# Gate weights applied in the expert loop instead of behind it, in a one-core Trainium2 mixture-of-experts kernel

## The reference

```
pg = softmax(x @ Wg + bg);  gw, gi = top_k(pg, 2)             # 2 groups
pe = softmax(x @ We[g] + be[g]);  ew, ei = top_k(pe, 1)       # 1 expert in each
h  = gelu(x @ W1 + b1);  oe = h @ W2 + b2
out = sum over the 2 groups of  gw * ew * oe[chosen expert]
y  = out @ Wp + bp
return (y - mean) * rsqrt(var + eps) * gamma + beta            # added to the residual h
```

## Time and profile before

| | us |
|---|---|
| median of 3 runs | 294.81 |
| lowest and highest | 291.74, 296.34 |
| the profiled execution | 292.14 |
| its span in the profile | 290.3 |
| PE, DVE, ACT, POOL busy in it | 244.0, 131.6, 117.6, 124.8 |
| granted TensorE clock, mean | 0.908 |

### The profile page before, as it was taken

One profiled execution on the slowest core, in us unless ns is written; L12 is line 12 of the kernel. 1 busy time (PEld: TensorE's weight loads), 2 busy tenths in 40 slices (PEclk: granted clock), 3 DMA queues, 4 the chain that ended last, 5 costly groups with the idle time before them and its releaser, 6 DMA issues.

```text
span 290.3 us, 8714 instructions
## 1 busy us (share of the span) xinstructions
PE 244.0 (84%) x3013; PEld 226.9 (78%) x3013; DVE 131.6 (45%) x491; ACT 117.6 (41%) x436; POOL 124.8 (43%) x152
## 2 busy tenths in 40 slices
PE   7889993307379999999999999999999999369860
PEld 6677762006379999999999999999999999359750
DVE  7638887897053352332233233223322322212796
ACT  4355566215023344334424433443343344235960
POOL 5775550840524447556655664455445422200000
PEclk9999998555559999999999999999999999975995
DMA  4411441417998983899265265992595210085023
GB/s 78 81 29 24 107 110 44 119 46 180 238 248 200 260 216 93 212 229 221 79 148 164 59 154 154 237 228 77 133 234 164 71 54 27 28 250 186 28 81 110
DMA packets 55035, 39.20 MB, mean 135 GB/s; under 512 B 30131, under 2 KB 52165, under 8 KB 55013
## 3 DMA queue, kind: packets, MB, share of 16 engines
q1 hardware_dynamic: 50004, 26.51, 38.6%
q0 software_dynamic: 5008, 12.43, 15.0%
HBM read 30.36 MB, written 8.55 MB: 134 GB/s over the span
## 4 chain that ended last, share of the span: by engine, by line
PE 54%; issue 16%; DVE 10%; POOL 7%; DMA 5%; ACT 5%; POOLq 0%; SPq 0%; DVEq 0%; ACTq 0%
PE pA L1223 21%; PE pY L1236 18%; POOL y_rows L506 3%; POOL xg L500 3%; DMA xg<-x_rows,token_of 2%; PE pY L1143 2%; PE pX L1210 2%; PE pA L1159 2%; DMA ys<-y_rows 2%; DVE ys L1012 2%; PE pY L1144 2%; DVE ys L1017 2%; PE pY L1167 1%; PE pY L1087 1%; PE pY L1044 1%
## 5 line engine op out<-in xcount | busy, mean ns | idle before, releaser
L653 ACT ACTIVATE hT<-pA,b_s 128x128 f32<-128x128 f32 x234 | 64.7, 375 | 112.7 <-PE pA L1223 112.7
L1223 PE MATMUL pA<-xs,W_s 64*128 64x128 f32 x1404 | 90.0, 279 | 0.9 <-DVE xs L947 0.8
L1223 PEld LDWEIGHTS pA<-xs,W_s 64*128 64x128 f32 x1404 | 84.7, 192 | 1.1 <-issue 1.1
L1236 PE MATMUL pY<-W_s,hT 64*128 64x192 f32 x936 | 83.8, 323 | 1.0 <-DVE yo L976 1.0
L1236 PEld LDWEIGHTS pY<-W_s,hT 64*128 64x128 f32 x936 | 76.4, 187 | 1.1 <-issue 1.1
L506 POOL DMA_INDIRECT y_rows<-yo,dest_of x39 | 38.6, 990 | 74.1 <-DVE yo L976 74.1
L974 DVE COPY yo<-pY 128x192 f32<-128x192 f32 x39 | 14.0, 358 | 107.4 <-PE pY L1236 107.4
L500 POOL DMA_INDIRECT xg<-x_rows,token_of x41 | 39.9, 973 | 25.8 <-issue 9.0
L947 DVE COPY xs<-pX 128x192 f32<-128x192 f32 x82 | 25.3, 350 | 12.3 <-PE pX L1210 9.3
L463 POOL TENSOR_SCALAR x<-h,mu,rs 128x192 f32<-128x192 f32 x16 | 16.5, 1038 | 16.4 <-DVEq L856 8.3
L1210 PEld LDWEIGHTS pX<-ident,xg 64*128 64x128 f32 x246 | 16.3, 141 | 5.9 <-issue 5.9
(11 more groups left out here) (241 smaller groups left out, 265.7 us busy)
## 6 DMA issues: line engine op xcount, KB each, us to landing
W_s<-in_L_ffn_W_dram SPq DMA_DIRECT2D x30, 288.0 KB, 4.3
W_s<-in_L_ffn_W_dram SPq DMA_DIRECT2D x15, 576.0 KB
x_rows<-x SPq DMA_DIRECT2D x16, 192.0 KB, 2.7
ys<-y_rows SPq DMA_DIRECT2D x8, 384.0 KB, 5.7
out_dram<-ys SPq DMA_DIRECT2D x8, 192.0 KB, 1.9
xg<-x_rows,token_of POOLq DMA_INDIRECT x41
y_rows<-yo,dest_of POOLq DMA_INDIRECT x39
emb<-n_L_tok_embed_table_dram,ids POOLq DMA_INDIRECT x16, 2.5
```

The costliest lines, as they stand in the source:

```text
L653: ins = nc.scalar.activation(hT[v][:, j * P:(j + 1) * P], units(v, j), ACT.Gelu, bias=b1_s[u][:, j:j + 1])
L1223: mm = pe.matmul(units(v, n * HB + j), W1_s[u][rows, g, j * P:(j + 1) * P], xs[v][rows, g, :], start=(g == 0 and j == 0), stop=(g == DG - ...
L1236: mm = pe.matmul(pY[n][:, 0:D], hT[v][rows, j * P:(j + 1) * P], W2_s[u][rows, j, :], start=(j == 0), stop=(j == HC - 1))
```

## The change

The gate weights are written to a small table in DRAM, `w_rows`, one float for each pair. For each expert tile POOL gathers its 128 weights into a column of `wt`, with `weight_of` as index (the pair's number, or 0 for an empty place). DVE's two evictions multiply by that column, so that `y_rows` holds weighted rows, and the end stage adds two rows, a pair of tiles in one operation. ACT's scaling in the end stage goes away; it takes the root straight from the sums of squares. The order of the end stage is written anew: the mixes of two groups ahead, then the roots of a group with scale-downs of the group before between its steps. TensorE does two fillers in each skipped step and 27 behind the loop, and no longer waits for `moe_done`.

```diff
+    w_rows = nc.dram_tensor("w_rows", [K * TOKENS, 1], F32).ap()
...
+        weight_of = sb("weight_of", [P, ST], I32)
+        wt = sb("wt", [P, SLOTS])
+        root_eps = sb("root_eps", [P, 1])
...
-        ROOT_AT = {hi + 4: (g, lo, hi) for g, (lo, hi) in enumerate(GROUPS)}
+        ROOT_AT = {hi + 2: (g, lo, hi) for g, (lo, hi) in enumerate(GROUPS)}
...
+        w_store = w_rows.rearrange("(k p i) o -> p k (i o)", k=K, i=NT)
...
                 load_w2(e, t)
+                if t == SLOTS - 2:
+                    with nc.allow_non_contiguous_dma(reason="64-byte rows of weights"):
+                        sp.wait_ge(wk_known, 1)
+                        sp.dma_start(w_store, wk[:, :, :]).then_inc(w_out, 16)
             def renew(t, v, free):
...
             loaded = pool.value_load(steps_loaded[0:1, 0:1], min_val=AHEAD, max_val=ST)
+            def fetch_weight(t):
+                u = t % SLOTS
+                pool.indirect_dma_start(wt[:, u:u + 1], None, w_rows, bass.IndirectOffsetOnAxis(
+                    ap=weight_of[:, t:t + 1].bitcast(U32), axis=0)).then_inc(wt_in[u], 16)
             gather(SLOTS)
+            pool.wait_ge(w_out, 16)
+            for t in range(SLOTS):
+                fetch_weight(t)
             gather(SLOTS + 1)
...
                         scatter(t)
+                if t + SLOTS < FULL * SLOTS:
+                    fetch_weight(t + SLOTS)
+                elif t + SLOTS < ST:
+                    with pool.If(used > t + SLOTS):
+                        fetch_weight(t + SLOTS)
                 if SLOTS <= t < SLOTS + NT:
...
             load_table(ACT.Sqrt)
-            def scaled(i):
-                act.wait_ge(ys_in[i // CB], 16)
-                nc.scalar.activation(ys[:, 0, i, :], ys[:, 0, i, :], ACT.Copy, scale=wk[:, 0, i:i + 1]).then_inc(y1w, 1)
             def turned_mix(j):
...
                 nc.scalar.activation(ys[:, 1, i, :], ps_y(i), ACT.Square, accum_out=ss3[:, i:i + 1]).then_inc(squared, 1)
-            for i in range(NT + 5):
+            for i in range(NT + 3):
+                if i < NT:
+                    turned_mix(i)
                 if i in ROOT_AT:
                     g, lo, hi = ROOT_AT[i]
-                    act.wait_ge(var3, g + 1)
-                    nc.scalar.activation(sd3_s[:, lo:hi], ve3[:, lo:hi], ACT.Sqrt).then_inc(sd3, 1)
-                if i < NT:
-                    scaled(i)
+                    act.wait_ge(squared, hi)
+                    nc.scalar.activation(sd3_s[:, lo:hi], ss3[:, lo:hi], ACT.Sqrt, bias=root_eps[:, 0:1],
+                                         scale=0.25 / D).then_inc(sd3, 1)
                 if 2 <= i < NT + 2:
-                    turned_mix(i - 2)
-                if 4 <= i < NT + 4:
-                    square(i - 4)
+                    square(i - 2)
         @block.vector
...
             nc.vector.memset(unit[:, :], 1.0)
+            nc.vector.memset(root_eps[:, :], 0.25 * EPS)
             nc.vector.memset(idle[:, :], 1.0).then_inc(idle_set, 1)
...
                 hot_lanes(lo, lo + GROUP // 2)
+            link(V.reciprocal(pmax_v, r4[:, :]))
+            link(V.tensor_tensor(pg1[:, :, :], second[:, :, :], lg_t[:, :, 0, :], ALU.mult))
+            link(V.tensor_reduce(gmax2[:, :], pg1[:, :, :], AX.X, ALU.add))
+            link(V.tensor_tensor(gmax2[:, :], gmax2[:, :], pmax[:, :, 0], ALU.mult))
             dve.wait_ge(inv_mm, 1)
...
             link(V.tensor_tensor(inv[:, 3, :], inv[:, 1, :], inv[:, 0, :], ALU.add))
+            V.tensor_scalar(weight_of[:, :], inv[:, 3, :], -1.0, 0.0, ALU.add, ALU.max)
             spare = dump[:, :, :].rearrange("p a b -> p (a b)")
...
             turned(0, 0)
-            link(V.reciprocal(pmax_v, r4[:, :]))
-            link(V.tensor_tensor(pg1[:, :, :], second[:, :, :], lg_t[:, :, 0, :], ALU.mult))
-            link(V.tensor_reduce(gmax2[:, :], pg1[:, :, :], AX.X, ALU.add))
-            link(V.tensor_tensor(gmax2[:, :], gmax2[:, :], pmax[:, :, 0], ALU.mult))
             for k, (group, gw) in enumerate(((first[:, :, 0, :], pmax[:, :, 0]), (second[:, :, :], gmax2[:, :]))):
...
                 link(V.tensor_tensor(wk[:, k, :], wk[:, k, :], gw, ALU.mult))
+            dve.sem_inc(wk_known, 1)
             turned(1, 1)
...
                 at_least(dve, sent[u], 16 * i)
-                V.tensor_copy(yo[u][:, :], pY[0][:, 0:D]).then_inc(y_half, 1)
+                dve.wait_ge(wt_in[u], 16 * (i + 1))
+                V.tensor_scalar(yo[u][:, :], pY[0][:, 0:D], wt[:, u:u + 1], None, ALU.mult).then_inc(y_half, 1)
                 dve.wait_ge(y_half, t + 1)
-                V.tensor_tensor(yo[u][:, :], pY[1][:, 0:D], yo[u][:, :], ALU.add).then_inc(y_ev, 1)
+                V.scalar_tensor_tensor(out=yo[u][:, :], in0=pY[1][:, 0:D], scalar=wt[:, u:u + 1], in1=yo[u][:, :],
+                                       op0=ALU.mult, op1=ALU.add).then_inc(y_ev, 1)
             for u in range(SLOTS):
...
             dve.wait_ge(resid, NT)
-            def mix(i):
-                dve.wait_ge(y1w, i + 1)
-                V.scalar_tensor_tensor(out=mixw[:, i, 0:D], in0=ys[:, 1, i, :], scalar=wk[:, 1, i:i + 1],
-                                       in1=ys[:, 0, i, :], op0=ALU.mult, op1=ALU.add).then_inc(mix_done, 1)
+            def mix(b):
+                tiles = slice(CB * b, CB * b + CB)
+                dve.wait_ge(ys_in[b], 16)
+                V.tensor_tensor(mixw[:, tiles, 0:D], ys[:, 0, tiles, :], ys[:, 1, tiles, :], ALU.add).then_inc(mix_done, CB)
             def scaled_down(i):
...
                     V.tensor_tensor(fin[:, tiles, :], fin[:, tiles, :], h2[:, tiles, :], ALU.add).then_inc(fin_done, 1)
-            pending = []
-            for i in range(NT + 5):
-                if i in ROOT_AT:
-                    g, lo, hi = ROOT_AT[i]
-                    dve.wait_ge(squared, hi)
-                    V.tensor_scalar(ve3[:, lo:hi], ss3[:, lo:hi], 0.25 / D, 0.25 * EPS, ALU.mult, ALU.add).then_inc(var3, 1)
-                if i < NT:
-                    mix(i)
-                for j in pending[0:2 if i >= NT else 1]:
+            def roots_of(g, lo, hi, older):
+                tiles = slice(lo, hi)
+                dve.wait_ge(squared, hi)
+                link(V.tensor_scalar(ve3[:, tiles], ss3[:, tiles], 0.25 / D, 0.25 * EPS, ALU.mult, ALU.add))
+                for j in older[0:2]:
                     scaled_down(j)
-                pending = pending[2 if i >= NT else 1:]
-                if i in ROOT_AT:
-                    dve.wait_ge(sd3, g + 1)
-                    link(V.reciprocal(rs3[:, lo:hi], sd3_s[:, lo:hi]))
-                    link(V.tensor_tensor(tn3[:, lo:hi], rs3[:, lo:hi], ve3[:, lo:hi], ALU.mult))
-                    link(V.tensor_tensor(tn3[:, lo:hi], tn3[:, lo:hi], sd3_s[:, lo:hi], ALU.add))
-                    link(V.reciprocal(rs3[:, lo:hi], tn3[:, lo:hi]))
-                    pending = pending + list(range(lo, hi))
-            for j in pending:
+                dve.wait_ge(sd3, g + 1)
+                link(V.reciprocal(rs3[:, tiles], sd3_s[:, tiles]))
+                for j in older[2:3]:
+                    scaled_down(j)
+                link(V.tensor_tensor(tn3[:, tiles], rs3[:, tiles], ve3[:, tiles], ALU.mult))
+                for j in older[3:4]:
+                    scaled_down(j)
+                link(V.tensor_tensor(tn3[:, tiles], tn3[:, tiles], sd3_s[:, tiles], ALU.add))
+                link(V.reciprocal(rs3[:, tiles], tn3[:, tiles]))
+            mix(0)
+            mix(1)
+            older = range(0)
+            for g, (lo, hi) in enumerate(GROUPS):
+                if g < 3:
+                    mix(hi // CB)
+                    mix(hi // CB + 1)
+                roots_of(g, lo, hi, older)
+                older = range(lo, hi)
+            for j in older:
                 scaled_down(j)
...
             mm.then_inc(inv_mm, 1)
-            def keep_busy(scratch):
-                for _ in range(BUSY):
+            def keep_busy(scratch, count=BUSY):
+                for _ in range(count):
                     pe.matmul(scratch, ident[:, :], ident[:, :], start=True, stop=True)
...
                         down(i * SLOTS + u, u, LOAD2 * (i + 1))
-            pe.wait_ge(moe_done, 1)
-            keep_busy(pA[1][:, 0:P])
+                    with pe.Else():
+                        keep_busy(pA[1][:, 0:P], 2)
+            keep_busy(pA[1][:, 0:P], 3 * BUSY)
             for i in range(NT + 1):
...
```

More of the change, by code:

```diff
@@ L299, in lm_tower @@
         w1_in = [sem(f"w1_in{u}") for u in range(SLOTS)]
+        wk_known, w_out = sem("wk_known"), sem("w_out")
+        wt_in = [sem(f"wt_in{u}") for u in range(SLOTS)]
         w2_in = [sem(f"w2_in{u}") for u in range(SLOTS)]
@@ L306, in lm_tower @@
         ys_in = [sem(f"ys_in{b}") for b in range(B)]
-        y1w, mix_done, mixT_mm, mixT_ev, proj_mm, fin_done, fin_out = (sem(n) for n in (
-            "y1w", "mix_done", "mixT_mm", "mixT_ev", "proj_mm", "fin_done", "fin_out"))
```

(2 more changed lines are left out.)

## The result

The change is slightly slower. In 15 runs of each kernel the median is 295.36 us (292.42 to 298.07) against 294.27 (289.03 to 296.34) for the kernel before: 1.1 us more. By both the change is slower, and by less than 2%. The profiled execution of the change took 293.85 us, 1.71 more than that of before. The forecast was 293.5, with 0.4% gained.

A forecast was written before the change was run, and what follows sets the result against it. TensorE was taken to pace the expert loop at 4.2 us a tile. Approach 0, loop and evictions +0.05 and the end stage's walk together gave 1.3 us less: from median 294.81 to 293.5 us, range 289.5 to 297.5.

The forecast's parts named there:

- (a): Approach: four chained DVE operations move ahead of the wait for the inverse table; cost nothing, 0.15 us to spare.
- (c): Approach: SyncE waits for wk before storing the table, holding slot 3's loads; cost taken as 0, bounds 0 and 2 us.
- (d): Approach: table store lands at about 86, POOL's four weight gathers push gather(5) to 91.1; in time by 1 us or more.
- (e): Before down(1): first weight lands between 88.6 and 93.3, needed by 92.4; stall 0 to 0.9 us, taken as 0.
- rival C: First weight holds the loop's start if its fetch lands after 92.4: 1 to 3 us, 294.5 to 296.5; chance 0.12.
- Loop: Expert loop: slower second eviction shows only in the last tile, +0.05 us; POOL's extra gathers cost 0, bound 1 us.
- (f): Behind the loop: 45 fillers end at about 260.5, first transpose possible at 259.3; cost 1.2 us on the path.
- The walk: End stage followed step by step: late mixes delay T12, DVE's last work ends at 286.7 against 288.02, 1.3 us less.
- (g): End stage: fillers give full clock; a tile takes TensorE 0.86 us instead of 1.71 at half clock.
- A: Larger gain: fillers also remove the spread from half clock in other executions, 290.8 or 290.2 us; chance 0.22.
- B: Clock still falls in the end stage, in pauses before T8 and T12: 296.8 to 297.9 us; chance 0.13.
- D: End stage: late mixes and filler overrun eat the gain, 294.8 us; chance 0.08.

The follow-up runs named there:

- b2: Kernel before plus table, store, weight gathers, DVE's waits and moved operations, weights unused, end stage and fillers as before: 291.43 us, ratio 1.0007.
- set B: The experiment set holding b1 to b4 with its own runs of the kernel before, whose median was 291.5 us.
- c4: Kernel before without an edit, run in a long set: ratio to itself 0.9967, end stage 34.4 us.
- d1: Kernel before without an edit, run in a long set: ratio to itself 1.0015, end stage 35.7 us.
- e1: Kernel before without an edit, run in a short set: median 291.83 us, ratio to itself 1.0003, end stage 35.7 us.
- short sets: Experiment sets B and E, in which the kernel before had medians of 291.5 and 291.4 us.
- e2: The change with each gather of 128 floats replaced by one of 128 rows of x, 768 bytes each: 295.34 us, ratio 1.018 to before.
- b4: b3 with the table's store moved from SyncE's DMA queue to ACT's: 290.21 us, ratio 0.9944 to before.
- b3: The change with all eight mixes ahead of the first roots and 17 fillers behind the loop instead of 27: 288.76 us, ratio 0.9933 to before.
- b1: The change itself, run once more: 295.63 us, ratio 1.0171 to before.
- c1: The change with 17 fillers behind the loop instead of 27, in a long set: ratio 1.1631 to before, end stage 35.2 us.
- d4: The change with only the four weight gathers ahead of the loop, later tiles reusing those weights, in a long set: 322.64 us, ratio 1.0293 to before.
- long sets: Experiment sets A, C and D, in which the kernel before had medians of 314.0, 313.0 and 315.0 us.

## Why the prediction was wrong

By its own steps:

- **Approach (a), (b), (c), (d).** Right in the sum: b2 costs nothing that can be seen. The store took 6.4 us until POOL's fetch instead of some 3, and gather(5) went at 94.29 instead of 91.1, with no stall behind it.
- **(e), the first weight.** The landing was rightly bounded (at 93.3 at the latest; it came by 93.14), the stall was wrongly taken as a constant 0, with 0.9 as its bound. It is 0 where down(0) comes late by the clock, and about 1.2 us where it comes as early as in the earlier trace rows. The condition of rival C, a fetch landing after 92.4, was met, and hidden by a slower up(1).
- **Loop.** +0.5 us for +0.05 predicted. Both evictions take 0.42 us instead of 0.36, not only the second, and TensorE's wait for them before the last down product is 0.3 us longer; the rest of the 0.5 is not traced.
- **(f), fillers.** T0 10.1 us behind the loop; predicted 10.44. Cost on the path 1.9 us; predicted 1.2, since the landing of the rows was taken over from before's profile, 1.2 us later than in the change's.
- **The walk.** From the loop's end to the last add 36.7 us predicted, 37.2 measured; the block of the second group 3.5 predicted, 3.57 measured; the pause before T12 2.8 predicted, 2.68 measured.
- **(g), the failed step.** "What they give is the clock: now 0.50 at 254 and again at 261, until about 267." I charged that stretch to every execution of before and set the walk against its 38.0 us, which also holds rows that landed late. That length belongs to one execution: five others of the same code took 34.1 to 36.2, of which 25.4 to 26.8 us from T0 on instead of 28.2. Against these the new end stage with its 37.1 to 38.0 us is 1 to 4 us slower, which is the size of what the medians show (1.1 us in the result's runs, 4.1 in set B). A walk of before's order with full clock from T0 on would have warned me; I made none. By b2 and c4 it ends some 4 us earlier than the one I compared with. The runs at hand gave a sign, too: one of the three others of before took 291.74, less than the profiled 292.14, and I wrote only of the two that were longer.
- **The profiled pair alone.** 290.9 predicted for the change's, 293.85 measured: 2.0 us of it from the start of down(0), 0.4 the loop, 0.5 the walk. Of the 2.0, 1.6 lie between up(0) and down(0), with up(1) at half clock, and 0.4 in the first gather's landing. From up(0) to down(0) before took 7.6, 7.0, 6.9 or 9.4 us (the profile, d1, c4, e1), and the kernels with gathers in short sets 7.5, 9.2, 9.2, 9.4, 9.5 and 9.5 (e2, after, b4, b2, b3, b1). So both lengths come with and without the gathers. That the gathers make the long one no more frequent isn't shown by these profiles; that b2 costs nothing in the medians speaks for chance.
- **Rivals.** A reasoned from the same stretch, in the wrong direction: the fillers take before's good executions away as well as the bad. B's half clock came, at 278 to 282. It cost nothing in the change's profile (27.1 us from T0 to the last add, as in c1, whose clock stayed full), and up to 0.9 us where it came earlier: 27.5 in d4, 27.9 in e2. C gave the right time, 294.5 to 296.5, by luck: its stall wasn't there in the change's profile. D's two causes were the right ones, 3.6 and 1.9 us, but were set against a gain that is mostly not there.

What b3 shows besides: the change's idea was sound. With mixes first and fillers cut, the same table of weights saves 2.8 us by the medians (ratio 0.9933, under the 2% that the prediction could hope to tell).

## What to carry to other kernels

Before a gain is booked on a stretch at half clock, see the same stretch in two or three executions of the unchanged kernel; here that baseline moved by 4 us and the forecast gain was 1.3. Fillers can hold the clock, but a pause behind them may lose it again, and they shorten nothing that waits for another engine: they pay only if they end before the first real operand is ready, so count them from that row. And when the order of an in-order engine is written anew, put what another engine waits for (the mixes) ahead of what only its own chain needs.

## What the runs showed of the hardware

A store of 128 x 2 rows of 64 bytes beside weight loads took 4.7 to 6.4 us to land from SyncE's queue (five profiles: the change's, b1, b2, b3, e2) and 8.6 from ACT's (one, b4). An indirect DMA of 128 single floats holds POOL as long as one of 128 rows of 768 bytes (0.94 us each, change and e2). Before ran on one chip in 313.0 us in one set and 291.4 in another; in the long sets a further gather in each turn made a turn 1.3 us longer, with TensorE idle for no semaphore, and in the short sets it cost nothing that can be seen (b2, ratio 1.0007). Behind the same 2.7 us pause of TensorE the clock fell to half after 0.3 us in one execution (e2), after 1.3 us in another (the change) and not at all in a third (c1).
